# Flamingo-style gated cross-attention and local-attention layers on one core: four pairs ahead of the repeating step, and q's squares folded once on GpSimd

## Chip, cores and metric

One NeuronCore of one Trainium2 chip. The metric is the device time of one execution in microseconds, as the median of several runs. The fast TensorE level is 2.4 GHz, the other 1.2 GHz; the profile gives the granted clock as a share of full speed.

## What is computed

Sixteen sequences `x[b]` of 128 tokens by 128 values go through a gated cross-attention and then, regrouped, through a two-layer block of local attention and feed-forward; the block's change is scaled by a second gate. Cut to what matters:

```python
# cross-attention, one head, per sequence, over 120 context rows of 96 values
a = layernorm(x); c = layernorm(ctx)
p = softmax((a@Wq+bq) @ (c@Wk+bk).T * 128**-0.5)
x = x + tanh(g_xattn) * ((p @ (c@Wv+bv)) @ Wo + bo)
# block: the sequence is normalised and transposed, then two layers of
h = shift_token(x);  q, k, v = split(h @ wqkv)            # 8 heads of 64
q, k = l2norm(q)*qs, l2norm(k)*ks;  q, k = rotary_xpos(q, k)
x = x + local_attention(q, k, v) @ wo                      # window 64
h = layernorm(shift_token(x));  a, g = split(h @ w1 + b1)
x = x + (a * gelu(g)) @ w2 + b2
```

`l2norm` divides each head's 64 values by the root of the sum of their squares: 16 sums (8 heads of q, 8 of k) per token.

## The kernel before

Everything lies in SBUF. The work is in units of one sequence in one layer, called a batch here: `m.i` from 0 to 31, the layer is `m.i // 16`. Buffers of a batch come in twos, by `m.i % 2`. The feed-forward works on groups of four batches (the last four in two groups of two), the cross-attention on pairs of sequences, eight in all.

Five engine programs (SP only loads and stores) run each in its own queue and in its own order, and meet by semaphores. Each has a function `step(s)`, called for `n` from -168 to 58, and in it a list of conditions, the order of which is the order of the queue. `s.on(d)` means that batch `n + d` exists; `s.pair(d)` gives a pair every other step, but only from pair `XP` on; `s.group(d)` a group every fourth step. What belongs to the pairs below `XP`, and to the last two groups, stands in lines of its own with a number (`if s.n == -25`). The number serves only to place the call in the queue: a call of step -25 runs as soon as its engine and its semaphores allow.

A batch goes through these functions (engine, line of the work):

- TensorE `project_k`, `project_q`, `project_v` (L505 to L507): h times the weights as a high and a low part, three matmuls of 512 columns each, into PSUM. `wqkv_hi` is made by ScalarE (`weights_high`, L1006), `wqkv_lo` by GpSimd (`weights_low`, L355). `h_hi` is a cast on VectorE (`token_high`, L1322; `group_high`, L1328), `h_lo` a subtraction on GpSimd (`token_low`, L392).
- ScalarE `squares(m, s)` (L1059) squares q (s=0) or k (s=1) into `sqr`. VectorE `turns(m, s)` (L1355, L1358) makes the two rotary products from PSUM, GpSimd `rotate(m, s)` (L410) adds them.
- VectorE `squared(m, s)` (L1365) sums the squares per head: 128x512 to 128x8. GpSimd `clamped(m)` (L423) limits the 16 sums from below, ScalarE `lengths(m)` (L1063, L1065) makes `rr`, their inverse roots. GpSimd `unit_k(m)` (L417) scales k by them; q's go in with the mask.
- TensorE `rows_q` (L634), `rows_k` (L644) transpose; ScalarE `q_rows` and VectorE `k_rows` (L1387) copy out; TensorE `scores_` (L661); VectorE `maxima_(m, a)` (L295 as its first mark, then L1376) scales, masks and takes row maxima; ScalarE `weights(m, a)` (L1071) the exponentials; VectorE `inverse`, GpSimd `normalise(m, a)` (L403), TensorE `weights_T` (L677), ScalarE `weights_out` (L1076), TensorE `attend` (L689) and `out_proj` (L698), VectorE `attn_residual`.
- Per group: `deviation`, `variance`, six `hidden` matmuls (L730), ScalarE `gelu` (L1102), VectorE `gate` (L1410), TensorE `back` (L780), VectorE `update`.

In step n VectorE sums q's squares of batch n+3 (`squared(s.at(3), 0)`) and k's of batch n+4; GpSimd does `unit_k(n+2)`, `rotate(n+2, 0)`, `rotate(n+3, 1)`, `clamped(n+3)`, `normalise(n+1, 0)` and `normalise(n+1, 1)`, with the cross-attention's parts between.

A pair of the cross-attention goes through: VectorE `stats(p)` (L1252), ScalarE `norms(p)` (L1011 to L1014), `tokens_normed` and `context_normed` (VectorE for pairs 0 and 1: L1277, L1284; GpSimd for the others: L375, L365), TensorE `tokens_T`, `context_T`, ScalarE `tokens_affine` (L1018), `context_affine`, then `query_in`/`query_out`, `context_scores`, VectorE `maxima(p)` (L1296), ScalarE `context_exps` (L1032), `values_in`/`values_out`, `probs_T`/`probs_out`, `mix`, VectorE `context_sums`, `residual`, ScalarE `norm_out`, `stack_in` (VectorE or GpSimd, L385), TensorE `out_T`, ScalarE `results`, then `token_high` and `token_low`, after which the pair's two batches can be projected. `weights_folded` (L486 to L489) and VectorE's `folded` (L1263) join the cross-attention's weights once; four `bias_fold` calls (L497, six matmuls of one column each) put the layernorm's bias through w1.

PSUM's eight banks are shared by all. Ahead of a matmul that writes a bank, `passed(semaphore, value)` waits for its last reader.

The parts of `XP` = 2 pairs stand in numbered lines; pairs 2 to 7 run in the repeating lines from step -19 (`stats`) to step 8. ScalarE needs two function tables; before, `gelu_and_others` is loaded ahead of a group's three gelus (L1199) and `natural_log_exp_and_others` right behind them (L1212).

Of the kernel before, what the change touches and what calls it, by code (L numbers as in the profile page):

```python
# [27 lines left out]
ALU = mybir.AluOpType  # L28
# [6 lines left out]
INNER = HEADS * DH  # L35
# [7 lines left out]
XP = 2  # L43
# [53 lines left out]
def build(nc, x, ctx_768, bo, wqkv, q_scale, k_scale, w1, wo, w2, packed, rot, mask, ident, out):  # L97
    ctx = ExitStack()
    with ctx:
# [87 lines left out]
        TT_B, CT_B, QI_B, VI_B, SC_B, PX_B, MI_B, OX_B = (TQ, TQ, SB), (OB, VB, VB), (SB, KB, KB), (SB, QB, VB), (TK, TQ, TQ), (OB, TQ, SB), (OB, KB, TK), (SB, TK, TQ)  # L187
# [6 lines left out]
        ld_x = [sem(f"ld_x{k}") for k in range(3)]  # L194
        ld_c = [sem(f"ld_c{k}") for k in range(3)]
# [19 lines left out]
        q_ps, k_ps, v_ps = (sem(n) for n in ("q_ps", "k_ps", "v_ps"))  # L215
        sqq_done, sqk_done, redq_done, redk_done, ss_ready, ln_done, r_ready = (
# [57 lines left out]
        FIRST, LAST = -168, 58  # L274
# [32 lines left out]
        XCH = CCH = ((0, 2), (2, 8), (8, 16))  # L307
# [3 lines left out]
        def _(sp):  # L311
# [24 lines left out]
        def _(pool):  # L336
            pool.dma_start(bo_s[:], bo.rearrange("(o d) -> o d", o=1)).then_inc(ld_b, 16)
            pool.dma_start(rott[:], rot).then_inc(ld_small, 16)
# [19 lines left out]
            def context_normed(p):  # L358

                pool.wait_ge(x_rs, 3 * p + 3)  # L360
                if p == XP:
                    pool.wait_ge(x_zc, XB * XP)
# [5 lines left out]
            def tokens_normed(p):  # L368

                pool.wait_ge(x_rs, 3 * p + 3)  # L370
                if p == XP:
                    pool.wait_ge(x_z, XB * XP)
# [5 lines left out]
            def stack_in(p):  # L378

                pool.wait_ge(x_rs2, 2 * p + 2)  # L380
                if p == XP:
                    pool.wait_ge(x_z2, XB * XP)
# [28 lines left out]

            def unit_k(m):
# [12 lines left out]
            def step(s):  # L425
                if s.n == -1:
                    weights_low(0, 2)
                if s.on(2):
                    unit_k(s.at(2))
                if s.pair(7) is not None:  # L430
                    stack_in(s.pair(7))
                if s.on(2):
                    rotate(s.at(2), 0)
                if s.pair(14) is not None:
                    tokens_normed(s.pair(14))
                if s.n == 8:
# [3 lines left out]
                if s.pair(13) is not None:  # L440
                    context_normed(s.pair(13))
                if s.n == -8:
                    token_low(0)
                if s.pair(6) is not None:
                    token_low(s.pair(6))
                if s.n == -63:
                    tables_(0)
                if s.on(3):
                    rotate(s.at(3), 1)
# [1122 lines left out]
```

## Time and profile before

| what | value |
|---|---|
| median of 3 runs | 400.29 us |
| lowest and highest run | 395.24, 403.95 us |
| the profiled execution | 399.71 us |
| its span in the profile | 397.9 us |
| TensorE, VectorE, ScalarE, GpSimd busy | 90%, 84%, 78%, 59% |

The span goes from the first to the last instruction that the profile shows; the profiled execution took 1.8 us more. PE is TensorE, PEld its weight loads, DVE VectorE, ACT ScalarE, POOL GpSimd. A line such as `26.26 0.26 DVE L1322 CAST h_hi<-xs ...` gives start, duration, engine, line of the kernel, operation, output and input; in brackets stands the idle time of the engine ahead of it and what ended it.

### The profile page before, as it was taken

To read this page: it belongs to the slowest core of one execution; us is meant where nothing else is said; L and a number is where in the kernel's file an instruction comes from. 1 tells how busy PE (TensorE), PEld (TensorE's weight loads), DVE (VectorE), ACT (ScalarE), POOL (GpSimd) and SP (SyncE) were. 2 spreads that over 40 slices of the span, in tenths; PEclk is the share of its full clock that TensorE was granted. 3 is DMA by queue.
4 is the path that set the end of the run, shared out by engine and by line. 5 is a ranking of instruction groups with operands and counts; after the bars stand their busy time and mean duration, and the time that the engine had idled before them with its cause. 6 is when DMAs were issued, how large, how long until landed. Compare 5 with 4: busy or idle time off the path is not lost.

```text
span 397.9 us, 8200 instructions
## 1 busy us (share of the span) xinstructions
PE 359.7 (90%) x2502; PEld 263.1 (66%) x2502; DVE 336.0 (84%) x1286; ACT 308.4 (78%) x976; POOL 235.3 (59%) x260
## 2 busy tenths in 40 slices
PE   2888669899999999999999999999999999999895
PEld 1676548677776767667666677667666766666663
DVE  3697797999986999998899889998999889975535
ACT  3575658898989879986897689868986898678852
POOL 2197777797756659757564755575557554662200
PEclk9966888999999999999999999999999999999999
DMA  8900000000000000000000000000000000000001
GB/s 227 331 4 0 2 1 2 2 2 2 2 1 2 0 2 0 2 2 1 2 0 2 2 2 2 1 2 1 2 2 0 2 1 2 29 0 2 27 2 53
DMA packets 3472, 7.14 MB, mean 18 GB/s; under 512 B 403, under 2 KB 1973, under 8 KB 3429
## 3 DMA queue, kind: packets, MB, share of 16 engines
q1 hardware_dynamic: 3005, 6.13, 4.6%
q0 software_dynamic: 144, 0.26, 0.4%
q8 instruction: 21, 0.34, 0.4%
q10 hardware_dynamic: 279, 0.22, 0.2%
q14 instruction: 23, 0.18, 0.1%
HBM read 5.57 MB, written 1.05 MB: 17 GB/s over the span
## 4 chain that ended last, share of the span: by engine, by line
PE 64%; DVE 19%; ACT 7%; issue 6%; DMA 2%; POOL 1%; SPq 0%; DVEq 0%; POOLq 0%
PE ps L730 8%; PE ps L689 7%; PE ps L698 6%; PE ps L661 5%; PE ps L780 5%; PE ps L677 4%; PE ps L505 4%; PE ps L507 4%; PE ps L506 4%; DVE pp L1376 3%; PE ps L644 3%; DVE sn L1358 3%; PE ps L634 3%; DVE cs L1355 3%; ACT pT L1076 2%
## 5 line engine op out<-in xcount | busy, mean ns | idle before, releaser
L1071 ACT ACTIVATE pp<-pp,nm 128x128 f32<-128x128 f32 x256 | 99.1, 392 | 3.0 <-DVE nm L1376 2.8
L410 POOL TENSOR_TENSOR cs<-cs,sn 128x512 f32<-128x512 f32 x64 | 82.2, 1299 | 0.0
L403 POOL TENSOR_TENSOR pp<-pp,pri 128x512 f32<-128x512 f32 x64 | 66.7, 1042 | 16.5 <-DVE pri L1383 14.3
L1376 DVE CUSTOM_DVE_ANT_0 pp<-ps,msk,rr 128x128 f32<-128x128 f32 x256 | 74.3, 346 | 0.4
L423 POOL TENSOR_SCALAR ssc<-ss 128x16 f32<-128x16 f32 x32 | 7.9, 248 | 99.9 <-DVE ss L1365 99.9
L1076 ACT ACTIVATE pT<-ps 128x512 f32<-128x512 f32 x64 | 34.8, 596 | 36.2 <-PE ps L677 36.1
L1071 ACT ACTIVATION_READ_ACCUMULATOR pp<-pp,nm 128x1 f32 x256 | 49.0, 191 | 0.0
L730 PE MATMUL ps<-hn,w1g 128*128 128x512 f32 (+3 forms) x108 | 47.8, 555 | 1.2 <-DVE sn L1358 0.9
L505 PE MATMUL ps<-wqkv_hi,h_hi 128*128 128x512 f32 x96 | 45.9, 478 | 2.7 <-DVE sn L1358 2.4
L1358 DVE TENSOR_TENSOR sn<-ps,stab 128x256 f32<-128x256 f32 x128 | 47.6, 413 | 0.0
L661 PEld LDWEIGHTS ps<-kT,qT 64*128 64x128 f32 x512 | 31.9, 191 | 21.9 <-issue 15.8
L1355 DVE TENSOR_TENSOR cs<-ps,ctab 128x512 f32<-128x512 f32 x64 | 43.9, 686 | 2.9 <-ACT sqr L1059 1.4
L689 PE MATMUL ps<-pT,vv 128*64 128x128 f32 x512 | 35.0, 277 | 8.9 <-ACT pT L1076 8.6
L1365 DVE TENSOR_REDUCE ss<-sqr 128x8 f32<-128x512 f32 x64 | 42.5, 665 | 0.0
L689 PEld LDWEIGHTS ps<-pT,vv 128*64 128x64 f32 x512 | 28.2, 136 | 21.2 <-issue 21.2
L1059 ACT ACTIVATE sqr<-ps 128x512 f32<-128x512 f32 x64 | 37.6, 588 | 3.6 <-PE ps L507 2.7
L661 PE MATMUL ps<-kT,qT 64*128 64x128 f32 x512 | 38.1, 289 | 1.5 <-DVE kT L1387 1.4
L507 PE MATMUL ps<-wqkv_hi,h_lo 128*128 128x512 f32 x96 | 38.9, 405 | 0.0
L506 PE MATMUL ps<-wqkv_lo,h_hi 128*128 128x512 f32 x96 | 38.8, 405 | 0.0
L698 PEld LDWEIGHTS ps<-oT,wo_raw 128*128 128x128 f32 x256 | 32.5, 192 | 7.0 <-issue 6.2
L417 POOL TENSOR_TENSOR cs<-cs,rr 128x512 f32<-128x512 f32 x32 | 33.5, 1048 | 2.9 <-ACT rr L1065 2.7
L677 PE MATMUL ps<-idn,pp 128*128 128x128 f32 x256 | 35.0, 279 | 0.2 <-ACT gl L1102 0.2
(132 smaller groups left out, 750.5 us busy)
## 6 DMA issues: line engine op xcount, KB each, us to landing
wqkv_raw<-in_L_ffn_wqkv_dram SPq DMA_DIRECT2D x2, 768.0 KB, 12.8
out_dram<-xt SPq DMA_DIRECT2D x3, 256.0 KB, 2.4
w_raw<-in_w_dram SPq DMA_DIRECT2D x1, 682.0 KB, 13.0
xt<-in_x_dram SPq DMA_DIRECT2D x1, 512.0 KB, 9.2
wo_raw<-in_wo_dram SPq DMA_DIRECT2D x1, 512.0 KB
xt<-in_x_dram SPq DMA_DIRECT2D x1, 384.0 KB, 6.4
ct<-in_ctx_dram SPq DMA_DIRECT2D x1, 360.0 KB, 10.0
ct<-in_ctx_dram SPq DMA_DIRECT2D x1, 270.0 KB, 6.8
```

The lines of the kernel that those rows point to most:

```text
L403: T(pp[m.j][:, a, :, :], pp[m.j][:, a, :, :], pri[m.j][:, a * 4:a * 4 + 4].unsqueeze(2).to_broadcast([128, PAIRS, 128]), ALU.mult).then_in ...
L410: T(cs[m.j][:, part], cs[m.j][:, part], sn[m.j][:, part], ALU.add).then_inc((aq_done, ak_done)[s], 1)
L505: mm(ps[:, part, :], hi, whi, start=True, stop=False)
L507: mm(ps[:, part, :], lo, whi, start=False, stop=True).then_inc((q_ps, k_ps, v_ps)[part], 1)
L661: last = mm(ps[:, SA + a, c * 128:(c + 1) * 128], qT[m.j][r, c, :], kT[m.j][r, c, :], start=True, stop=True)
L689: last = mm(ps[a * 64:a * 64 + 64, OB, c * 128:(c + 1) * 128], vv[m.j][:, h * DH:(h + 1) * DH], pT[m.j][:, a, c, :], start=True, stop=True)
L698: last = mm(ps[:, OB, Y], wo_raw[:, m.layer, c, :], oT[m.j][:, c, :], start=(c == 0), stop=(c == PAIRS - 1))
L730: mm(ps[0:m, bank, t.w], w1g[:, layer, s * HID + o:s * HID + o + m], hg, start=True, stop=True).then_inc((ha_ps, hg_ps)[s][c], 1)
L1071: A(pp[m.j][:, a, c, :], pp[m.j][:, a, c, :], ACT.Exp, bias=nm[m.j][:, a * 4 + c:a * 4 + c + 1], scale=-1.0, accum_out=psum_[m.j][:, a * 4 ...
L1355: V.tensor_tensor(heads(cs[m.j], s), x_, ctab[:, m.layer, s, :].unsqueeze(1).to_broadcast([128, HEADS, DH]), ALU.mult)
L1358: last = V.tensor_tensor(heads(sn[m.j], s)[:, :, o_], x_[:, :, i_], stab[:, m.layer, s, o_].unsqueeze(1).to_broadcast([128, HEADS, 32]), A ...
L1376: last = V.tensor_tensor_reduce(out=pp[m.j][:, a, c, :], in0=ps[:, SA + a, c * 128:(c + 1) * 128], in1=msk[:], scale=rr[m.j][:, h:h + 1], ...
```

## The change

It has five parts.

1. `XP` goes from 2 to 4, so that pairs 2 and 3 too stand in numbered lines. The order of the numbered lines is new on all engines, the PSUM banks of the pairs are new (a fifth set of banks for the repeating lines), and with them the `passed` waits: eight go, one comes ahead of `rows_q`, and the numbered lines have others. `VP = 2` keeps the split between VectorE and GpSimd at pair 2.

```diff
-XP = 2
+XP = 4
-        FIRST, LAST = -168, 58
+        FIRST, LAST = -155, 58
...
             def rows_q(m):
                 pe.wait_ge(aq_done, m.i + 1)
                 passed(pt_ready[0], min(m.i - 1, ALL))
+                passed(qT_ready, min(m.i, ALL))
                 passed(x_out, 2 * pairs_by(m.i + 5))
                 passed(x_p, XB * pairs_by(m.i + 6))
```

2. The loads: chunks of 1, 1, 2 and 4 pairs instead of 1, 3 and 4; SP and GpSimd wait for the first pair before they issue the rest; wqkv of layer 0 goes ahead of the last chunk.

```diff
+        VP = 2
-        XCH = CCH = ((0, 2), (2, 8), (8, 16))
+        XCH = CCH = ((0, 2), (2, 4), (4, 8), (8, 16))
...
-            for k in range(1, 3):
+            sp.wait_ge(ld_x[0], 16)
+            sp.wait_ge(ld_c[0], 16)
+            for k in range(1, 4):
+                if k == 3:
+                    sp.dma_start(wqkv_raw[:, 0, :], wqkv[0]).then_inc(ld_w[0], 16)
                 sp.dma_start(*rows(xt, x, XCH[k])).then_inc(ld_x[k], 16)
                 sp.dma_start(*rows(ct, ctx_768, CCH[k])).then_inc(ld_c[k], 16)
-            sp.dma_start(wqkv_raw[:, 0, :], wqkv[0]).then_inc(ld_w[0], 16)
...
             pool.dma_start(bo_s[:], bo.rearrange("(o d) -> o d", o=1)).then_inc(ld_b, 16)
+            pool.wait_ge(ld_c[0], 16)
             pool.dma_start(rott[:], rot).then_inc(ld_small, 16)
```

3. The fold. GpSimd adds the upper 32 squares of each head of q to the lower 32, in place, and VectorE sums 32 values per head: 128x256 to 128x8. k's sums stay as they are.

```diff
+            def squares_folded(m):
+                pool.wait_ge(sqq_done, m.i + 1)
+                q = sqr[m.j][:, 0:INNER].rearrange("p (h d) -> p h d", d=DH)
+                T(q[:, :, 0:DH // 2], q[:, :, 0:DH // 2], q[:, :, DH // 2:DH], ALU.add).then_inc(fold_q, 1)
...
             def squared(m, s):
-                dve.wait_ge((sqq_done, sqk_done)[s], m.i + 1)
-                V.tensor_reduce(ss[m.j][:, s * HEADS:(s + 1) * HEADS], heads(sqr[m.j], s), AX.X, ALU.add).then_inc(
+                dve.wait_ge((fold_q, sqk_done)[s], m.i + 1)
+                sq = heads(sqr[m.j], s)
+                V.tensor_reduce(ss[m.j][:, s * HEADS:(s + 1) * HEADS], sq if s else sq[:, :, 0:DH // 2], AX.X, ALU.add).then_inc(
                     (redq_done, redk_done)[s], 1)
```

4. GpSimd's step has the fold of batch n+3 behind `rotate(n+2, 0)`; the three `weights_low` of layer 1 go from step 8, ahead of `rotate(n+3, 1)`, to step 11, behind it. `context_normed` of pairs 4 to 7 is two steps later than before (`pair(13)` to `pair(11)`), `stats` one (`pair(24)` to `pair(23)`), VectorE's `w1_in(1)` goes from step 13 to 9. The orders near the loop's start, after the change (a few of the calls, with their step):

```
GpSimd   -155 tables_(0)  -25 tokens_normed(2)  -18 context_normed(2)  -12 weights_low(0,1)
         -10 weights_low(0,0) token_low(0) weights_low(0,2)  -9 context_normed(3)  -8 tables_(1)
         -6 tokens_normed(3)  -5 tokens_normed(4) token_low(1)  -3 squares_folded(0) tokens_normed(5) rotate(0,1) clamped(0)
         -2 unit_k(0) stack_in(2) rotate(0,0) squares_folded(1) context_normed(4) rotate(1,1) clamped(1)
VectorE  -50 stats(0)  -45 centring() folded()  -44 tokens_normed(0)  -35 context_normed(0)  -29 stats(1)
         -2 turns(1,0) bias_sum turns(2,1) squared(1,0) k_rows(0) token_high(2) squared(2,1)
         -1 maxima(3) maxima_(0,0) turns(2,0) maxima_(0,1) ... 
ScalarE  -77 norms(0)  -68 norms(1)  -51 tokens_affine(0)  -50 context_affine(0)  -46 query_out(0)
TensorE  -6 bias_fold(0,0) bias_fold(0,1) out_T(1)  -5 project_k(0)
```

Before, VectorE has `stats(0)`, `stats(1)`, `tokens_normed(0)` in step -43, and in step -2 `k_rows(0) squared(2,1) token_high(2)`; GpSimd has `weights_low(0,2)` first in step -1.

5. ScalarE's table loads come from a helper: `table(name)` loads only when the other table is in, ahead of the next function that needs it. Behind a group's gelus the load of the logarithm's table now stands behind `squares(n+4, 1)` and ahead of `weights`.

## Rows read from the trace of the kernel before

**Rows 1.** The page, part 1: busy time of each engine, share, instructions.

```profile
PE 359.7 (90%) x2502; PEld 263.1 (66%) x2502; DVE 336.0 (84%) x1286; ACT 308.4 (78%) x976; POOL 235.3 (59%) x260
```

**Rows 2.** Stages: stretch, length, busy PE, PEld, DVE, ACT, POOL; PE clock, DMA share, GB/s.

```profile
20.00:40.00 20.00, 16.77 (x70) 14.21 (x71) 16.70 (x76) 12.62 (x44) 16.38 (x26) 0.64 0.01 2
40.00:60.00 20.00, 12.94 (x73) 10.02 (x72) 17.68 (x56) 12.42 (x44) 15.52 (x18) 0.84 0.00 1
65.00:105.00 40.00, 37.02 (x326) 30.67 (x327) 38.85 (x161) 35.95 (x130) 32.53 (x38) 1.00 0.01 2
...
246.74:286.90 40.16, 39.24 (x283) 27.73 (x283) 36.83 (x136) 32.77 (x105) 24.30 (x26) 1.00 0.00 1
```

**Rows 3.** Groups by line; count, busy us, mean ns, idle us before, releaser.

```profile
L1365 DVE TENSOR_REDUCE ss<-sqr 128x8 f32<-128x512 f32 x64 | 42.5, 665 | 0.0
...
L417 POOL TENSOR_TENSOR cs<-cs,rr 128x512 f32<-128x512 f32 x32 | 33.5, 1048 | 2.9 <-ACT rr L1065 2.7 <-issue 0.2
...
L1199 ACT ACT_TABLE_LOAD x7 | 9.0, 1283 | 0.1
...
L423 POOL TENSOR_SCALAR ssc<-ss 128x16 f32<-128x16 f32 x32 | 7.9, 248 | 99.9 <-DVE ss L1365 99.9
...
L392 POOL TENSOR_TENSOR h_lo<-xs,h_hi 128x256 fp32r<-128x256 f32 x8 | 5.4, 681 | 1.4 <-DVE h_hi L1322 1.4
...
L1296 DVE TENSOR_REDUCE nmx<-ps 128x2 f32<-128x240 f32 x8 | 3.2, 403 | 3.4 <-PE ps L581 3.4
```

**Rows 4.** DMA issues: count, KB each, median us from issue to landing.

```profile
wqkv_raw<-in_L_ffn_wqkv_dram SPq DMA_DIRECT2D x2, 768.0 KB, 12.8
...
idn<-in_identity_dram SPq DMA_DIRECT2D x1, 64.0 KB, 3.3
```

**Rows 5.** Timeline from 6 to 30 us: start, duration, instruction, idle before.

```profile
6.50 0.74 PE L489 MATMUL ps<-bo_s,hot 1*97 1x128 f32 x2
...
9.03 0.29 DVE L1252 BATCH_NORM_STATS2 bst<-xt 128x6 f32<-128x128 f32 x1 [2.87 <-DMA ct<-in_ctx_dram]
...
10.17 0.57 DVE L1277 TENSOR_SCALAR hn<-xt,mv,r 128x128 f32<-128x128 f32 x2
...
10.80 0.20 ACT L1014 ACTIVATE r<-lnv 128x4 f32<-128x4 f32 x1
...
11.58 0.56 ACT L1018 ACTIVATE x1T<-ps,first 128x256 f32<-128x256 f32 x1 [0.58 <-PE ps L551]
...
18.06 1.14 ACT L1006 ACTIVATE wqkv_hi<-wqkv_raw 128x512 fp32r<-128x512 f32 x2
...
29.31 0.78 PE L505 MATMUL ps<-wqkv_hi,h_hi 128*128 128x512 f32 x1
```

**Rows 6.** Timeline, VectorE's two casts and what follows the second.

```profile
26.26 0.26 DVE L1322 CAST h_hi<-xs 128x256 fp32r<-128x256 f32 x1
...
48.52 3.60 DVE L1322 CAST h_hi<-xs 128x256 fp32r<-128x256 f32 x1
...
50.67 1.29 POOL L410 TENSOR_TENSOR cs<-cs,sn 128x512 f32<-128x512 f32 x1
...
51.93 1.64 POOL L375 TENSOR_SCALAR hn<-xt,mv,r 128x128 f32<-128x128 f32 x2
...
57.06 1.09 PE L634 MATMUL ps<-idn,cs 128*128 128x128 f32 x4 [1.57 <-ACT xp L1032]
...
63.30 0.06 DVE L295 MEMSET mark_v<- 128x1 f32 x1 [1.49 <-PE ps L661]
```

**Rows 7.** Timeline of GpSimd: clamped in two early steps, and a middle step.

```profile
88.68 0.25 POOL L423 TENSOR_SCALAR ssc<-ss 128x16 f32<-128x16 f32 x1
...
97.91 0.25 POOL L423 TENSOR_SCALAR ssc<-ss 128x16 f32<-128x16 f32 x1 [2.64 <-DVE ss L1365]
...
259.29 2.51 POOL L410 TENSOR_TENSOR cs<-cs,sn 128x512 f32<-128x512 f32 x2
...
264.14 0.24 POOL L423 TENSOR_SCALAR ssc<-ss 128x16 f32<-128x16 f32 x1 [2.34 <-DVE ss L1365]
```

More of the change, by code:

```diff
@@ L431, in step @@
                     stack_in(s.pair(7))
+                if s.n == 0:
+                    stack_in(3)
+                if s.n == -10:
+                    weights_low(0, 0)
+                if s.n == -2:
+                    stack_in(2)
+                if s.n == -8:
+                    tables_(1)
+                if s.n == -1:
+                    token_low(2)
                 if s.on(2):
                     rotate(s.at(2), 0)
+                if s.on(3):
+                    squares_folded(s.at(3))
+                if s.pair(6) is not None:
+                    token_low(s.pair(6))
+                if s.n == -10:
+                    token_low(0)
+                if s.pair(11) is not None:
+                    context_normed(s.pair(11))
+                if s.n == -6:
+                    tokens_normed(3)
+                if s.n == -25:
+                    tokens_normed(2)
+                if s.n == -9:
+                    context_normed(3)
                 if s.pair(14) is not None:
                     tokens_normed(s.pair(14))
-                if s.n == 8:
+                if s.n == -12:
+                    weights_low(0, 1)
+                if s.on(3):
+                    rotate(s.at(3), 1)
+                if s.n == -18:
+                    context_normed(2)
+                if s.n == -155:
+                    tables_(0)
+                if s.n == 11:
                     weights_low(1, 0)
@@ L1109, in step @@
                 if s.n == 51:
-                    nc.scalar.preload_act_table_set("gelu_and_others")
                     gelu(8, 0)
+                if s.n == -10:
+                    weights_high(0, 2)
                 if s.n == -8:
-                    results(0)
+                    norms(3)
+                if s.n == -7:
+                    norm_out(1)
                 if s.on(4):
@@ L1174, in step @@
                     gelu(7, 0)
+                if s.n == -46:
+                    query_out(0)
+                if s.n == -1:
+                    norm_out(3)
                 if s.n == 58:
                     gelu(8, 2)
+                if s.n == -27:
+                    context_affine(1)
+                if s.n == -8:
+                    results(0)
+                if s.n == -51:
+                    tokens_affine(0)
                 if s.pair(10) is not None:
@@ L1488, in step @@
                     context_sums(s.pair(8))
+                if s.n == 0:
+                    token_high(3)
                 if s.on(1):
                     inverse(s.at(1), 1)
+                if s.n == -1:
+                    context_sums(3)
+                if s.n == -11:
+                    stack_in(1)
+                if s.n == -3:
+                    context_sums(2)
+                if s.n == -44:
+                    tokens_normed(0)
+                if s.n == -8:
+                    token_high(1)
+                if s.n == -3:
+                    residual(2)
+                if s.n == -2:
+                    token_high(2)
+                if s.n == -1:
+                    residual(3)
                 if s.on(4):
@@ L1494, in step @@
                     normed_h(7)
+                if s.n == -19:
+                    maxima(1)
                 if s.n == 45:
                     result(7)
[L1497 to L1498 removed]
                 if s.pair(7) is not None:
                     token_high(s.pair(7))
[L1501 to L1505 removed]
+                if s.n == 9:
+                    w1_in(1)
+                if s.n == -50:
+                    stats(0)
                 if s.pair(8) is not None:
```

440 lines of the change are left out of this document (248 added, 192 removed).

## The prediction

> **What bounds the kernel now.** I read the page first: TensorE is busy 90% of the span, VectorE 84%, ScalarE 78%, GpSimd 59% [rows 1]. An average over the span says little here, so I cut the span into stages [rows 2]. In the repeating step far from both ends (246.74 to 286.90 us, four steps in 40.16 us) TensorE is busy 39.24 us: only 0.92 us of four steps is not matmul, while VectorE has 3.3 us and GpSimd nearly 16 us free; the granted clock is 1.00. That stage, some twenty steps, is bound by TensorE. From 65 to 105 us it is the other way round: VectorE 38.85 of 40 us, TensorE 37.02. There the cross-attention pairs lie on top of the step and VectorE is the bound. From 20 to 60 us nobody is full: TensorE 29.7 of 40 us at a granted clock of 0.64 and 0.84, VectorE 34.4, and part of VectorE's time is not work, as shown below. So the change can earn in three places, in this order: the crossing into the loop (20 to 65 us), the VectorE-bound steps, and least in the long middle.
>
> **The fold, per step.** VectorE's sum over 512 values takes 665 ns; the nearest smaller sum is over 240 values, 403 ns [rows 3]. That is (665-403)/272 = 0.96 ns per value, so 256 values are 0.42 us and one sum saves 0.25 us, 32 times: 7.9 us of VectorE's busy time. GpSimd gets 32 new additions of 128x256. The nearest row is the other two-input operation of that size, L392, 681 ns; half of L417 (1048 ns) gives 0.52, and a strided access could make it as dear as a 128x512 addition, 1.26 us (2.51 for two [rows 7]). I take 0.66 us: 21 us more for GpSimd, from 235 to 256 us.
>
> Is the fold hidden? It stands behind unit_k and rotate(q), ahead of rotate(k). In a middle step GpSimd ends both rotates at 259.29+2.51 = 261.80 and then sits until 264.14, 2.34 us, for VectorE's sum [rows 7]; over the run that wait is 99.9 us in 29 of 32 steps, 3.4 us each [rows 3]. The squares are ready a step earlier, so the fold would end at about 261.2 and VectorE's sum, now at about 263.4, does not wait for it. Its cover is that idle time; without it 0.66 us would stand ahead of VectorE's sum, and behind that on VectorE the inverses and copies for which TensorE waits. In steps where GpSimd also has stack_in and context_normed the cover is gone: at 88.68 clamped starts with no wait, as GpSimd has only just ended its rotate [rows 7], so there it comes up to 0.7 us later.
>
> What does 0.25 us give? In the VectorE-bound stage, 65 to 105 us, up to its full size: four steps, 1.0 us (bounds 0 and 2.0, if all eight steps with pairs give it). In the middle only what TensorE's idle time allows: 0.92 us per four steps is an upper end of 5.5 us over 24 steps, but VectorE is not what the matmuls mostly wait for there; I take 0.1 us per four steps, 0.6 us (bounds 0 and 5.5).
>
> **The start of the loads.** SP now waits for the first pair's two loads. Behind that wait stand all other x and ctx chunks, the weights, the mask and later the stores; behind GpSimd's new wait stand the three small loads for the tables. The first pair's data are there at about 4.5 to 4.9 us, so pairs 1 to 3 and wqkv are asked for then and not at 1.6 to 3.5 us. The landing of a small load was 3.3 us after its issue [rows 4], so pair 1 is there at about 8.2 us; now its statistics start at 9.03 after 2.87 us of waiting for ctx [rows 5]. No loss. The first wqkv took 12.8 us to land; issued at 6.3 us instead of 3.5 and still taking that long, it would land at 19.1, and ScalarE reads it at 18.06 [rows 4, 5]: at worst 1.0 us late. But 874 KB of x and ctx now come behind it, so I take 0. The x and ctx of pairs 4 to 7 and w1, behind it, are first used after 20 us, mask and wo after 50.
>
> VectorE's order gains more on paper: tokens_normed(0) no longer stands behind stats(1) and can follow folded, whose matmuls end at 6.50+0.74 = 7.24 us. With 0.85 us for folded it starts at 8.1 instead of 10.17: 2.1 us [rows 5]. But ScalarE's queue takes it back. norms(1) stands ahead of tokens_affine(0) there, before and after the change, and it needs stats(1), which VectorE now does after context_normed(0), from 9.3 us. From stats(1) to the last of norms(1) it is 9.03 to 11.00 now, 1.97 us, so tokens_affine(0) starts at about 11.3 instead of 11.58. I take 0.3 us (bounds -1.0 and 3.1, the wait of 2.87 and a little earlier landing).
>
> From there to the first project_k (29.31) I find nothing that adds up. out_T(0) comes about 1 us earlier, since norm_out(0) is no longer behind norms(2) and probs_out(1). But results(0) now has weights_high(0,2), norms(3) and both affines of pair 2 ahead of it on ScalarE, and two bias folds stand directly ahead of project_k(0).
>
> **The crossing into the loop.** Two things stand out. First, VectorE's cast token_high(2) at 48.52 took 3.60 us; the same cast at 26.26 took 0.26 [rows 6]. During the 3.34 us between, VectorE does nothing and GpSimd runs without a gap (weights_low(0,2), unit_k, rotate), until tokens_normed at 51.93. VectorE's next work, the first masked maxima, starts when the cast ends, and TensorE stands behind that. In the new order weights_low(0,2) is done long before, and the cast comes before squared(2,1) while GpSimd is about to wait for the lengths. I expect a stall of about 1.1 us there, the rest of context_normed and rotate: gain 2.2 us (bounds 0 and 3.3).
>
> The Trainium skill, SBUF — State Buffer, in Who interferes with whom, says that a cast in a two-port mode and a GpSimd instruction exclude each other for one whole instruction, whoever came first, and that tensor_reduce never contends. By it the cast would wait for one GpSimd instruction, at most 1.3 us, and the gain of this term would be 2.0 us or more; the row, in which three GpSimd instructions went by, gives the lower end 0. The page speaks against the change as a whole, since every fold is one more holder of the pair.
>
> Second, rows_q(1) waited at 57.06 for the exponentials of pair 3 (the 1.6 us idle before it), and TensorE then ran at the lower of its two levels: its four transposes took 1.09 us and VectorE waited 1.49 us at 63.30 for the scores [rows 6]. With four pairs ahead this wait does not exist for pair 3, and maxima(3) goes before maxima_(0). I take 1.2 us (bounds 0 and 1.5). The bank changes and the added wait on qT_ready ahead of rows_q hit buffers long free: 0. results(3), ahead of rows_q(2), I put at 0 too (at most the 1.6 us that such a wait cost at 57.06).
>
> **Small moves.** The three weights_low of layer 1 (1.26 us each, 3.8 in all) go from step 8 to step 11, between rotate(k) and clamped, where GpSimd has 2.34 us less 0.66 free: clamped, and with it lengths and both normalise, come up to 2.1 us late once. I take a loss of 0.4 us (bounds 0 and 2.1). w1_in(1) and the pairs' stats move on engines with room: 0. ScalarE's table loads stay as many, each at its first user, where squares now precede the load: 0, with a rival below.
>
> **The sum.** 0.3 + 2.2 + 1.2 + 1.0 + 0.6 - 0.4 = 4.9 us. The profiled execution took 399.71 us (span 397.9 and 1.8 around it), which gives 394.8; from the median of the runs, 400.29, it would be 395.4. I forecast **395.0 us**. The runs themselves lie from 395.24 to 403.95, so about 2% (8 us) is what a measurement can tell from no change.
>
> **The rivals.**
> A, the forecast: 395.0, its own range 391.5 to 398.5. Chance 0.50.
> B, the loop begins earlier by the whole of what the front has: the 3.1 us of the front, 3.3 of the cast, 1.5 of the wait at 63.30, 2.0 of the folds, less 0.4: 9.5 us, 390.2. For it: TensorE's slow clock in 20 to 40 us stretches each delay, and a fuller front could lift it [rows 2]. Against it: norms(1) on ScalarE, and GpSimd, 16.38 of 20 us busy from 20 to 40 us, with weights_low(0,2), a second table and a fold more ahead of the first rotate. Chance 0.22.
> C, given back: the loop starts some microseconds earlier, and GpSimd, with 32.53 + 4 x 0.66 = 35.2 of 40 us, becomes late in the steps with pairs: clamped comes late, lengths behind it on ScalarE holds the squares, and the steps lose what the front won. About 399.7. For it: 88.68. Against it: in the step after, at 97.91, it waits 2.64 us again, and a pair spans two steps. Chance 0.17.
> D, slower: VectorE waits in its queue for the fold. In the twelve steps -3 to 8 the fold is not hidden: 12 x 0.66 = 7.9 us plus the 0.4, against 0.3 + 3.4 + 0.6 from the front and middle: +4.0, 403.7. It decides where GpSimd has less than 0.66 us idle before clamped in these steps. With a fold of 1.26 us it would be 15.1 in place of 7.9, 410.9. Chance 0.08.
> E, the change does not do what it says on ScalarE: squares now run with the gelu table loaded, which no row of before shows, so a load may be put ahead of them and another for the exponentials. Seven places at 1.28 us [rows 3] are 9.0 us; on the path they give 399.7 - 4.9 + 9.0 = 403.8. Chance 0.03.
> The Trainium skill, ScalarE: Activation LUTs, in What ACT_TABLE_LOAD costs, puts a switch at 2.66 us with its drain, which would make E's seven places 18.6 us (an estimate), and in Table sets names relu, copy, identity and abs as part of every set, not square.
>
> **Range and chances.** B's centre must be inside and D's too: 389.0 to 402.5 leaves about 2 in 10 out. Faster by over 2% means under 392.3: most of B and a little of A, 0.25. Slower by over 2% means over 408.3: D with the dear fold and mishaps not listed, 0.05. Within 2%: 0.70.
>
> **What would show it.** Right: sums of q at about 0.42 us and folds at about 0.66; four middle steps still in about 40 us with TensorE busy 39.2; token_high(2) under 1.5 us; no wait ahead of rows_q(1); the first maxima_ of batch 1 near 59.5 instead of 63.34. x1T of pair 0 near 11.3 tells A from B. Wrong: sums of q that wait for fold_q (D), ScalarE holding more than seven loads of each kind at the gelus (E), clamped without any wait in most early steps and 65 to 105 us holding no more work than now (C), or a middle cycle far from 40 us, since then TensorE was not the bound that I take it for.

## The result and the profile after

The changed kernel takes 394.72 us in the median of 20 runs (393.16 to 398.06), against 399.25 us for the kernel before in 20 runs on the same chip (394.67 to 405.3). The ratio is 0.994, with a 95% interval from 0.991 to 0.997: a small gain, inside the 2% that counts as no change. (The ratio leaves out runs over 1.5% above the fastest of their kernel, seven of the 20 before and none after, so it speaks of 2.4 us where the medians speak of 4.5.) The profiled executions are 393.99 us (span 392.2) after and 399.71 us (span 397.9) before.

Part 1 of the page after, busy time by engine, answers to [rows 1]:

```profile
PE 354.7 (90%) x2502; PEld 259.2 (66%) x2502; DVE 330.2 (84%) x1286; ACT 307.1 (78%) x976; POOL 257.2 (66%) x292
```

The groups by line (count, busy us, mean ns, idle before and its releaser), beside [rows 3]:

```profile
L1487 DVE TENSOR_REDUCE ss<-sqr 128x8 f32<-128x512 f32 x64 | 34.0, 531 | 0.0
...
L422 POOL TENSOR_TENSOR sqr<-sqr 128x256 f32<-128x256 f32 x32 | 23.5, 735 | 0.0
...
L1443 DVE CAST h_hi<-xs 128x256 fp32r<-128x256 f32 x8 | 12.5, 1568 | 0.2 <-ACT xs L1138 0.2
...
L435 POOL TENSOR_SCALAR ssc<-ss 128x16 f32<-128x16 f32 x32 | 8.2, 255 | 74.5 <-DVE ss L1487 74.4
```

VectorE's sums fell from 42.5 to 34.0 us: the 32 sums of k still take about 0.66, those of q 0.40 to 0.41. GpSimd has 32 additions of 0.735 us more and its idle time ahead of clamped went from 99.9 to 74.5 us, that is by about the folds. But VectorE's busy time fell by 5.8 us only and not by 8.5. The third line has the reason: the eight casts take 12.5 us together, where they took 8.1 before. Their mean of 1.57 us hides that two take nearly 4.5 us and the other six 0.26 to 0.91. (Some smaller VectorE work became about 2 us shorter.)

The stages after (columns as in [rows 2]):

```profile
20.00:40.00 20.00, 15.85 (x71) 13.10 (x72) 16.16 (x74) 12.94 (x42) 18.26 (x25) 0.67 0.13 47
40.00:60.00 20.00, 15.81 (x126) 12.43 (x125) 18.22 (x76) 15.55 (x56) 18.80 (x23) 0.99 0.01 2
...
65.00:105.00 40.00, 36.57 (x288) 29.69 (x286) 38.72 (x149) 33.79 (x121) 33.70 (x40) 0.96 0.00 1
246.74:286.56 39.82, 38.99 (x284) 27.69 (x282) 35.78 (x134) 32.69 (x105) 27.15 (x29) 1.00 0.01 1
```

From 40 to 60 us TensorE does 2.9 us more than before, at a clock of 0.99 in place of 0.84. From 65 to 105 us it does 0.5 us less, at 0.96 in place of 1.00. Four middle steps are 39.82 us, 0.34 less than the four of [rows 2], which contained a slow one; other groups of four differ by 0.2.

The best ruler for the rest is the start of the scores matmuls of each step (L661 before, L685 after). The span falls into five stretches:

| from the traces, us | before | after | difference |
|---|---|---|---|
| start to scores(3) | 81.41 | 73.11 | -8.30 |
| scores(3) to (8) | 52.40 | 57.99 | +5.59 |
| scores(8) to (16) | 83.21 | 81.79 | -1.42 |
| scores(16) to (31) | 148.94 | 148.13 | -0.81 |
| scores(31) to the end | 31.92 | 31.18 | -0.74 |
| span | 397.9 | 392.2 | -5.7 |

A step is named here by the scores at its end: step 5 runs from scores(4) to (5). The code's own numbers, which some of the expectations use, are three lower. Most of what the start wins is lost again in steps 5 (9.90 us before, 13.30 after) and 7 (12.77 and 15.15). The timeline of the first of these, after (start, duration, instruction, idle before and its releaser; here and below, lines of other work that stand between are left out):

```profile
81.22 2.05 POOL L409 TENSOR_TENSOR pp<-pp,pri 128x512 f32<-128x512 f32 x2
...
81.86 4.47 DVE L1443 CAST h_hi<-xs 128x256 fp32r<-128x256 f32 x1
83.22 1.06 POOL L429 TENSOR_TENSOR cs<-cs,rr 128x512 f32<-128x512 f32 x1
84.22 1.29 POOL L416 TENSOR_TENSOR cs<-cs,sn 128x512 f32<-128x512 f32 x1
85.45 0.73 POOL L422 TENSOR_TENSOR sqr<-sqr 128x256 f32<-128x256 f32 x1
86.26 0.60 DVE L1520 TENSOR_TENSOR xs<-ps,xs 64x128 f32<-64x128 f32 x2
86.41 0.72 POOL L398 TENSOR_TENSOR h_lo<-xs,h_hi 128x256 fp32r<-128x256 f32 x1 [0.23 <-DVE h_hi L1443]
...
87.00 1.09 PE L713 MATMUL ps<-pT,vv 128*64 128x128 f32 x16 [2.13 <-DVE xs L1520]
...
88.20 0.40 ACT L1158 ACTIVATE pp<-pp,nm 128x128 f32<-128x128 f32 x1 [2.69 <-DVE nm L1498]
```

Read it from the cast. It is issued inside GpSimd's first normalise, and stays until GpSimd comes to rest: both normalise, unit_k, rotate and the new fold go by. GpSimd rests only because token_low needs the result of this very cast. TensorE then waits 2.13 us for VectorE's residual and ScalarE 2.69 us for the next maxima. The same happens at 104.05, 4.49 us. In the kernel before the casts of those pairs took 0.79 and 0.78 us, and the long one was that of [rows 6].

### The profile page after: what moved, and what is told of

The parts are those of the page before. It is cut to its first block, busy times and chain, and to the rows that moved or that the text cites. A ratio compares the mean times of both kernels' runs of the same rounds, so it can differ in the third digit from the quotient of the medians.

```text
span 392.2 us, 8237 instructions
## 1 busy us (share of the span) xinstructions
PE 354.7 (90%) x2502; PEld 259.2 (66%) x2502; DVE 330.2 (84%) x1286; ACT 307.1 (78%) x976; POOL 257.2 (66%) x292
## 4 chain that ended last, share of the span: by engine, by line
PE 64%; DVE 17%; issue 8%; ACT 8%; POOL 1%; DMA 1%; ACTq 0%; DVEq 0%; POOLq 0%
PE ps L754 10%; PE ps L713 7%; PE ps L722 6%; PE ps L685 5%; PE ps L804 5%; PE ps L536 4%; PE ps L701 4%; PE ps L537 4%; PE ps L538 4%; PE ps L668 3%; PE ps L659 3%; DVE sn L1479 2%; DVE pp L1498 2%; ACT pT L1163 2%; DVE cs L1476 2%
## 5 line engine op out<-in xcount | busy, mean ns | idle before, releaser
L435 POOL TENSOR_SCALAR ssc<-ss 128x16 f32<-128x16 f32 x32 | 8.2, 255 | 74.5 <-DVE ss L1487 74.4
L685 PEld LDWEIGHTS ps<-kT,qT 64*128 64x128 f32 x512 | 31.1, 187 | 21.1 <-issue 11.3
L685 PE MATMUL ps<-kT,qT 64*128 64x128 f32 x512 | 37.2, 285 | 0.7 <-ACT qT L1171 0.5
L1487 DVE TENSOR_REDUCE ss<-sqr 128x8 f32<-128x512 f32 x64 | 34.0, 531 | 0.0
```

Of the source, the lines that this page charges most:

```text
L685: last = mm(ps[:, SA + a, c * 128:(c + 1) * 128], qT[m.j][r, c, :], kT[m.j][r, c, :], start=True, stop=True)
```

## The experiments

The runs came in three batches and one single run, each on a chip of its own. The kernel before ran in each, at 399.47, 400.0, 400.12 and 397.58 us. Medians of different batches can differ by that much without a cause in the kernel; the stretches between scores are the finer measure. Each ratio is to the kernel before of the same batch.

**The changed kernel again.**

> The changed kernel itself, as the yardstick of this batch. Its profile is expected at 392 to 394 us of span, ahead of the kernel before by about 8 us at the scores of batches 3 and 4, and with the casts token_high(4) and token_high(5) at about 4.5 us each instead of 0.8. If these two long casts were an accident of one execution, one or both are 0.8 us here and the span is 3 us shorter for each.

395.23 us in 10 runs, ratio 0.994 (0.990 to 0.998). The long casts come again, 4.45 us at 83.76 and 4.47 at 105.92. They are no accident of one execution.

**The fold alone.** The kernel before, with the fold behind rotate of q and nothing else of the change:

```diff
             def squared(m, s):
-                dve.wait_ge((sqq_done, sqk_done)[s], m.i + 1)
+                dve.wait_ge((fold_q, sqk_done)[s], m.i + 1)
...
                 if s.on(2):
                     rotate(s.at(2), 0)
+                if s.on(3):
+                    squares_folded(s.at(3))
```

> The kernel before with the fold alone. If the fold is worth what VectorE gains in the VectorE-bound steps and 0.2 to 0.3 us per four middle steps, it gains 1 to 3 us against before. Rival 1: in the early steps the fold makes GpSimd's queue gapless and VectorE's casts starve more often; then one or more token_high casts are over 3 us long and the gain is lost, 0 to +6 us. Rival 2: the fold does nothing to the time, within 0.5 us.

399.02 us in 10 runs, ratio 1.0036 (1.0001 to 1.0071): the fold alone gains nothing and rather costs a little. Its timeline has two long casts where the kernel before has one:

```profile
67.03 4.12 DVE L1331 CAST h_hi<-xs 128x256 fp32r<-128x256 f32 x1
...
88.86 4.46 DVE L1331 CAST h_hi<-xs 128x256 fp32r<-128x256 f32 x1
```

The long cast of [rows 6] is gone: that cast takes 0.32 us here, the small scaling after it 0.56 us, and the step from scores(0) to (1) 10.96 us in place of 12.80. The cast at 67.03 lengthens step 3 from 10.54 to 12.79 us instead. From scores(3) to (8) it needs 55.58 us, 3.18 more than before; from (8) to (31) 1.15 less. So the fold does gain 0.2 to 0.3 us in one step of four, and pays for it with each cast that it sets back.

**The change without the fold.** VectorE sums 64 values of q again, the rest of the change stays:

```diff
-                if s.on(3):
-                    squares_folded(s.at(3))
...
-                dve.wait_ge((fold_q, sqk_done)[s], m.i + 1)
+                dve.wait_ge((sqq_done, sqk_done)[s], m.i + 1)
```

> The changed kernel without the fold: sums over 64 values again. If the whole gain is the new order and the w1_in move, it stays at the changed kernel's time plus 1 to 3 us. If the fold is what starves the casts of pairs 4 and 5, those two casts fall to 0.8 us and it is 1 to 4 us faster than the changed kernel. If the starving comes from the order of the other GpSimd work, the casts stay at 3.5 us or more, shorter than 4.5 only by the fold's 0.7.

390.05 us (389.48 to 390.21, 4 runs), ratio 0.982 (0.977 to 0.987). No cast is longer than 0.79 us, and scores(3) to (8) takes 52.47 us, as before. With the result above it says that the order, the loads, w1_in(1) and the table loads together are worth about 9 us by the medians (7 by the ratio), and that the fold takes about 5 of them back: from scores(3) to (8) it is 5.5 us.

**The casts on ScalarE.** The changed kernel with its fold; ScalarE does the casts of pairs 4 to 7 behind heads_out:

```diff
+            def token_high(p):
+                act.wait_ge(x_out, 2 * p + 2)
+                at = slice(p * XB, p * XB + XB)
+                A(h_hi[:, at, :], xs[:, at, 0:N], ACT.Copy).then_inc(xh_hi, 1)
```

> The changed kernel with the casts of pairs 4 to 7 on ScalarE. If the long casts cost what the trace suggests (3.4 us in step 3's matmuls and 2.4 in step 5's), it is 4 to 6 us faster than the changed kernel, 389 to 391 us, and stays 8 us ahead of before until the scores of batch 7. Rival: VectorE's lost time is caught up later because TensorE is the bound from step 4 on; then it gains under 1 us.

389.79 us (388.53 to 390.39, 4 runs), ratio 0.981 (0.976 to 0.987). On ScalarE a cast takes 0.41 us, with GpSimd at work beside it, and steps 5 and 7 are 10.11 and 12.77 us. So it is VectorE's casts and not GpSimd's extra work as such: GpSimd does the same 32 folds here.

**GpSimd's order alone.** Nothing is added or taken away; token_low, which waits for the cast, goes from behind the fold to the head of GpSimd's step:

```diff
             def step(s):
+                if s.pair(6) is not None:
+                    token_low(s.pair(6))
                 if s.on(2):
                     unit_k(s.at(2))
...
-                if s.pair(6) is not None:
-                    token_low(s.pair(6))
```

> The kernel after, with one change: in GpSimd's step token_low(pair) stands first, ahead of unit_k, rotate of q and the fold, so that GpSimd comes to wait for VectorE's cast four instructions earlier. Nothing is added or removed. If a cast gets through only when GpSimd's queue comes to rest, the two casts of 4.5 us (pairs 4 and 5) end right behind the two normalise instructions, at 1.5 to 2.5 us each, and the kernel gains 3 to 5 us: 390 to 392 us. If a cast needs a fixed time or a given number of GpSimd instructions whatever the order, they stay at 4.4 us or more and the time stays at 394 to 396. If GpSimd becomes late by the wait, its sums of halves and clamps come later and steps 2 and 4 stay long with short casts: also 394 or more, but VectorE then waits at the sums of q.

389.01 us (388.61 to 390.08, 4 runs), ratio 0.975 (0.966 to 0.983). The cast arrives at the same place as after (81.87, in the first normalise) and ends with the second, as the first theory said:

```profile
81.23 2.03 POOL L409 TENSOR_TENSOR pp<-pp,pri 128x512 f32<-128x512 f32 x2
...
81.87 1.54 DVE L1443 CAST h_hi<-xs 128x256 fp32r<-128x256 f32 x1
...
83.49 0.73 POOL L398 TENSOR_TENSOR h_lo<-xs,h_hi 128x256 fp32r<-128x256 f32 x1 [0.23 <-DVE h_hi L1443]
84.18 1.04 POOL L429 TENSOR_TENSOR cs<-cs,rr 128x512 f32<-128x512 f32 x1
```

This is the clearest of the runs: same work, same arrival, and three instructions of GpSimd fewer in the run behind it make the cast 2.9 us shorter. From scores(3) to (8) it takes 52.96 us in place of 57.99, so the one moved call gains 5 us in this stretch. By the medians it is 6 us, somewhat more than expected, but these come from two batches.

**The same with five rounds, and its twin without the fold.** Both were run to price the fold where no cast is held for long.

> The version with token_low first on GpSimd once more, unchanged (389.01 us there), beside the one without the fold below. It should stand at 388.5 to 389.8, both casts at 1.5 to 1.6 us again. If the cast's length depends on where in GpSimd's run it happens to arrive and not on the order, one of the two can be back at over 3 us.

389.2 us (388.54 to 389.96, 6 runs), ratio 0.976 (0.973 to 0.979); the casts 1.53 and 1.57 us.

> token_low first on GpSimd, and no fold (VectorE sums 64 values of q again): the fold's own worth where the casts do not starve. The fold shortens one step in four of the middle by 0.18 to 0.2 us and steps 20, 24, 29 and a few of the early ones likewise, some 1.5 us of the span in all; so without it 390.0 to 391.0 us, 1 to 2 above the version with the fold. If GpSimd's extra 23.5 us of work cost as much as they save, both are within 0.5 us of each other.

390.94 us (389.65 to 391.98, 6 runs), ratio 0.980 (0.976 to 0.984). The medians say that the fold is worth 1.7 us. The stretches say 0.68: 0.48 lost from scores(3) to (8), 0.47 and 0.69 won in the two after that. The rest lies ahead of scores(3), where executions differ among themselves. So the sign is the expected one and the size is between 0.6 and 1.7 us.

**No fold, casts on ScalarE.** The version with the ScalarE casts, less the fold:

> The kernel after without the fold (VectorE sums 64 values of q again) and with the casts of pairs 4 to 7 on ScalarE behind heads_out. The fold is priced where nothing starves. If a hidden fold is worth the 0.12 us that each sum loses in the steps that VectorE bounds, this stands 0.5 to 2 us above the version with the ScalarE casts and the fold (389.8 us), at 390.3 to 391.8, with steps 20, 24 and 29 at 10.32 to 10.46 in place of 10.1 to 10.3. If the fold costs even there, through GpSimd's chain or the port, it stands under 389.5. Moving the casts alone, without the fold, should do nothing against the version without the fold (390.05): they took 0.4 to 0.8 us there.

391.75 us (389.37 to 392.65, 4 runs), ratio 0.980 (0.972 to 0.988). From scores(3) to (31) it is 283.42 us, against 282.82 with the fold: 0.6 us for the fold again. Its median is 1.7 us above the version without the fold whose casts stayed on VectorE, which the stretches do not show (283.42 against 283.60); four runs with a spread of 3.3 us can't tell.

**Less the waits at the loads.** From that version, the waits on the first pair's loads ahead of the later ones go:

```diff
-            sp.wait_ge(ld_x[0], 16)
-            sp.wait_ge(ld_c[0], 16)
...
-            pool.wait_ge(ld_c[0], 16)
             pool.dma_start(rott[:], rot).then_inc(ld_small, 16)
```

> The version of this call without the fold and with the ScalarE casts, less the three waits ahead of the later loads (SyncE no longer waits for the first pair of x and of the context before it issues the next pieces, GpSimd no longer waits before it issues the tables). If the early start comes from the first pieces having the DMA queues to themselves, stats(1), the first tokens_affine and x1T come 0.8 to 1.5 us later (x1T near 11.5 in place of 10.5) and the whole becomes 0.5 to 1.5 us longer. If it comes from the order of VectorE's and ScalarE's instructions alone, x1T stays within 0.3 us of 10.5 and the time within 0.3 us.

390.02 us (389.1 to 391.85, 4 runs), ratio 0.977 (0.970 to 0.984). x1T of pair 0 starts at 10.70 instead of 10.48, within the 0.3 us of the second theory, so its early start comes from the order. On the whole time these runs say little: the median fell by 1.7 us, in a spread of 3 us, while in the profiled execution scores(3) came 2.6 us later, with the clock lower from 40 to 60 us (0.83 against 1.00). From scores(3) to (31) the two agree within 0.13 us. No gain from the waits is shown. The new chunks of the loads, and wqkv ahead of the last one, were not undone in any run.

**w1_in(1) back in the code's step 13.** The base is again the version with neither the fold nor VectorE's casts:

```diff
-                if s.n == 9:
-                    w1_in(1)
...
+                if s.n == 13:
+                    w1_in(1)
```

> The version of this call without the fold and with the ScalarE casts, with w1_in(1) back in VectorE's step 13 as in the kernel before. If the w1_in of step 13 is what makes step 16 long (11.26 us before against 10.12 after), step 16 grows by 0.9 to 1.3 us here, step 9 or its neighbours shrink by at most 0.3, and the time grows by 0.7 to 1.2 us. If w1_in is covered wherever it stands (that is how it was predicted, at nothing), step 16 grows by under 0.3 and the time does not move.

Step 16 grows from 10.32 to 11.25 us, the size of the first theory, and its row says how:

```profile
198.41 1.58 DVE L1467 TENSOR_SCALAR w1g<-w_raw,first 128x682 f32<-128x682 f32 x1
...
202.51 0.30 PEld L752 LDWEIGHTS ps<-hn,w1g 128*128 128x128 f32 x2 [1.10 <-DVE sn L1485]
```

The median, 390.48 us (390.11 to 390.91, 4 runs), is not above that of its base (391.75), so 0.93 us is shown by the steps alone, and the expected growth of the whole time is not. From scores(8) to (16) it is 82.62 against 81.67, and every kernel of this study with w1_in(1) in the code's step 13 has the long step 16 (11.25 or 11.26 us, 10.91 with the fold alone; 10.12 to 10.33 in the others).

**The one cast of the kernel before.** The kernel before, with the cast of pair 2 on ScalarE behind heads_out:

```diff
                 if s.on(0):
                     heads_out(s.at(0))
+                if s.pair(7) == 2:
+                    token_high(2)
```

> The kernel before, with one instruction moved: the cast of pair 2, which took 3.60 us on VectorE at 48.52, is done by ScalarE behind heads_out of that step. If that cast is the greater part of what the crossing into the repeating steps gained (6.6 us from scores(0) to scores(1), by the traces before and after), the step from scores(0) to scores(1) falls from 12.80 us to 9.3 to 10.5 and the whole gains 2.2 to 3.3 us: 396 to 397 where before is at 399.5. If the gain came from the order of pairs 2 and 3 and of the last exps, whose waits stand right behind the cast, the step loses under 1 us and the time stays within 1 us of before.

399.26 us (395.99 to 403.21, 12 runs), ratio 0.9975 (0.993 to 1.002). The first theory fails, and what the second one said came: the step loses 0.94 us, and the time stays within 1 us of the kernel before in its batch (400.12). The cast takes 0.42 us on ScalarE and maxima_(0) goes ahead at 48.21, but the next VectorE instruction of this kind takes over the stall. It is the scaling of two columns for the pair's softmax, 0.17 us by itself:

```profile
52.04 0.72 POOL L392 TENSOR_TENSOR h_lo<-xs,h_hi 128x256 fp32r<-128x256 f32 x1
52.10 1.91 DVE L1306 TENSOR_SCALAR nmb<-nmx 128x2 f32<-128x2 f32 x1
52.72 1.26 POOL L410 TENSOR_TENSOR cs<-cs,sn 128x512 f32<-128x512 f32 x1
...
54.04 0.36 ACT L1032 ACTIVATE xp<-ps,nmb 128x120 f32<-128x120 f32 x1 [2.86 <-DVE nmb L1306]
...
54.98 0.30 PE L634 MATMUL ps<-idn,cs 128*128 128x128 f32 x1 [3.31 <-ACT xp L1032]
```

rows_q(1) now waits 3.31 us for the exponentials of pair 3, where it waited 1.57 in [rows 6]. The step from scores(0) to (1) falls from 12.80 to 11.86 us only. Two stalls lay one behind the other. In the changed kernel both are small: 0.91 us for the cast, and no wait ahead of rows_q(1). No run takes both away in the old order by themselves. The nearest is the fold alone, where both were short by the time at which they came, and this step took 10.96 us.

**Both remedies at once.** token_low first and the casts on ScalarE:

> Both remedies at once: the casts of pairs 4 to 7 on ScalarE and token_low first in GpSimd's step. If what was left of the casts (1.5 us twice) is still on the path, step 5 falls from 10.66 to about 9.9 to 10.1 us and the time to 388.2 to 388.8, 0.5 to 1 below token_low first alone (389.1). If TensorE or ScalarE sets the end of those steps, the two remedies do not add and it stands at 388.8 to 389.8.

389.18 us (388.53 to 392.28, 7 runs), ratio 0.980 (0.977 to 0.984). Step 5 falls from 10.66 to 10.07 us and step 9 from 11.85 to 11.35, but steps 4, 6 and 8 grow by 0.3 each: scores(3) to (8) is 53.24 against 52.96. The remedies do not add. From scores(3) to (31) the three versions with the fold and a remedy stand within 0.13 us: 282.89 with token_low first, 282.82 with the casts on ScalarE, 282.77 with both. token_low first is the smallest edit, at 389.0 and 389.2 us, ahead of both kernels.

## Why the prediction was right, and where its steps were not

The time came out at 394.72 for a forecast of 395.0. The nearness is luck, since two errors cancel: the start won more than the sum said, and a loss of 5.5 us was not in it. The gain itself, forecast at 4.9 us, is 4.5 by the medians, 2.4 by the ratio and 5.7 in the profiled pair.

**The front, 0.3 us.** Too low. x1T of pair 0 started at 10.52 and not at 11.3:

```profile
8.65 0.28 DVE L1373 BATCH_NORM_STATS2 bst<-xt 128x6 f32<-128x128 f32 x1
...
10.52 0.55 ACT L1101 ACTIVATE x1T<-ps,first 128x256 f32<-128x256 f32 x1
...
27.18 0.78 PE L536 MATMUL ps<-wqkv_hi,h_hi 128*128 128x512 f32 x1
...
44.38 0.91 DVE L1443 CAST h_hi<-xs 128x256 fp32r<-128x256 f32 x1
```

The mechanism (ScalarE's norms(1) holds x1T back until stats(1)) was right: from stats(1) to x1T it is 1.87 us. The term was mis-sized because stats(1) started at 8.65 and not from 9.3, with no wait for ctx; folded took 0.50 us where the working had 0.85. "Nothing that adds up" between there and project_k(0) was wrong too: that came at 27.18 instead of 29.31, 1.1 us more than x1T explains. By scores(0) the profiled pair is 3.6 us apart (44.72 against 48.27). The worst-sized term of the sum is this one. (The working's 874 KB behind wqkv are 512 and 360, so 872; nothing hangs on it.) The sentence that x1T near 11.3 tells A from B spoke for B, rightly: this part went as in B.

**The crossing, 2.2 + 1.2 us.** The cast took 0.91 us, under the 1.5 of the prediction, rows_q(1) has no wait, and maxima_ of batch 1 came at 56.15 where I had said 59.5 and the kernel before has 63.34. In the profiled pair the start to scores(3) is 8.3 us shorter against the 3.7 of the three terms. Of the 8.3, 3.6 lie ahead of scores(0) and 4.7 behind it, where the two crossing terms had 3.4. Part of this is the two executions: TensorE's granted clock was 0.50 from 56.5 to 63 us before and 1.00 after. The other kernels tell more: scores(3) came between 72.74 and 76.54 us in the eleven profiled executions with the new order (mean 74.0), and at 81.41, 80.11 and 78.25 in the three with the old one (mean 79.9). So the new order with its loads is worth about 6 us, some 2.8 ahead of scores(0) and 3.1 from there to scores(3). That is an estimate from few executions, and two of the three old ones hold a change of their own: the fold's held cast costs the second 2.2 us in step 3, and the moved cast helps the third. By it the two crossing terms together were right in size, and the front term was 2.5 us too small. The split into 2.2 for the cast and 1.2 for the wait behind it did not hold. The cast alone gives 0.9 us in its step, since the next stall takes over; that both together give the rest is argued from the traces, not shown by a run.

**The fold in the steps that VectorE bounds, 1.0 us.** This step failed. The fold costs 5.5 us there in the changed kernel (57.99 us from scores(3) to (8), 52.48 without it), where even the lower bound was 0. It costs 3.2 us in the old order. I put the fold's cover at GpSimd's idle time, found that time gone in steps with pairs, and priced it as clamped coming up to 0.7 us later. The price was not there but at VectorE: GpSimd's run without rest became the time that the cast waits. [rows 6] had the mechanism in it, a cast of 3.60 us over three GpSimd instructions, and the text counted only its disappearance at the crossing, not that it could come back elsewhere. The prediction also remarked that every fold is "one more holder of the pair", and gave this neither a price nor a chance. TensorE's clock is not the cause of the loss: in the profiled execution it was 0.50 from 88.5 to 91.5 us, in the repeat 1.00 through the whole stretch, and the repeat takes 57.95 us there too. Even where no cast is held for long the fold does not gain in this stretch: it loses 0.3 to 0.5 us. Rival C named the stage and the size (what the front wins is given back), and its sign came true: clamped starts without a wait, or with one of 0.14 us, in seven of the first eight steps after, and in two before, and 65 to 105 us hold no more work. Yet its mechanism, clamped that comes late, is not the cause: with token_low first clamped stands in the same place (81.02 us against 81.00) with as little wait, and the loss is gone.

The Trainium skill, SBUF — State Buffer, in Who interferes with whom, has the kind of conflict: a cast or a tensor_scalar on VectorE and a GpSimd instruction exclude each other when the VectorE one runs in a two-port mode, for the whole instruction of whoever comes first. No trace shows the mode. The traces agree on which operations suffer (the cast here, the tensor_scalar of two columns in the run on the kernel before, never the sums, which took 0.64 to 0.68 us over 512 values in both kernels), and differ on the size: the cast waited over up to five GpSimd instructions, 4.2 us beyond its own 0.26, where one instruction would have been 1.0.

**The fold in the middle, 0.6 us.** Right in kind and low by half: 0.2 us in one step of four, 1.15 us from scores(8) to (31) by the fold alone, 1.16 by the pair with token_low first. It is near the lower end of 0 to 5.5, as TensorE was the bound. The fold took 0.735 us against 0.66, the sum 0.41 against 0.42.

**The small moves.** The three weights_low of layer 1, taken at -0.4, cost nothing visible. w1_in(1), taken at 0, gives 0.93 us: in the code's step 13 it takes 1.58 us and TensorE waits for VectorE behind it, in step 9 it takes 1.00. The table loads, taken at 0 with a rival below it, give 0.74 us at the end. Both kernels have 19, two at the start and 17 in the steps, so E did not come. Before and after, the load ahead of the last group's variance (start, duration):

```profile
384.34 1.28 ACT L1195 ACT_TABLE_LOAD   x1
...
385.64 0.38 ACT L1089 ACTIVATE dsq<-ps 128x256 f32<-128x256 f32 x1
```

```profile
379.50 0.38 ACT L1176 ACTIVATE dsq<-ps 128x256 f32<-128x256 f32 x1
379.91 1.28 ACT L1079 ACT_TABLE_LOAD   x1
```

Before, the load stands between the gelus and the squares; after, the squares go first, and the matmul over them starts 1.1 us earlier counted from scores(31). That is read from the traces and the code; no run undid this part alone. The stretch behind scores(31) is 31.89 to 31.92 us in all three kernels with the old loads and 31.16 to 31.18 in all with the new ones.

**The sum as it was:** about 6 us from the order at the start (8.3 in the profiled pair), -5.6 from the casts (the pair's difference), 1.1 from the fold from step 8 on, 0.9 from w1_in(1), 0.74 from the table load at the end. That gives 3.1 by the mean of the starts and 5.4 in the profiled pair, where the spans differ by 5.7. The 4.5 of the medians and the 2.4 of the ratio lie on both sides of the first.

## What to carry to other kernels

When work moves to GpSimd, look for VectorE casts and small SBUF-only operations that are issued while GpSimd runs its two-input operations back to back; the cost lands on VectorE, and only the duration column shows it (a cast of 4.47 us where others have 0.26). Look for such a cast in the kernel before, too: it shows that the mechanism is there. If the cast's own consumer on GpSimd can go ahead of the run, its wait gives GpSimd the pause that lets the cast in; here that one moved call was worth 5 to 6 us, and the fold itself at most 1.7.

## What the runs showed of the hardware

A VectorE cast from SBUF to SBUF beside GpSimd's two-input operations can be passed over, not for one instruction, but until GpSimd pauses or comes to an operation of another kind. With the fold alone, the cast at 67.03 ended at 71.15, behind the fold and as GpSimd's tokens_normed, a TENSOR_SCALAR, began at 70.97; so did the cast of [rows 6].

Whether it is passed over goes with the time at which it is issued. In the traces of this study, 14 casts of pairs were issued 0.63 to 0.68 us before the end of such a GpSimd instruction that had another directly behind it: all 14 got in at that end and took 0.78 to 0.83 us, and the GpSimd instruction behind took 1.07 to 1.10 us. Nine were issued 0.39 to 0.43 us before such an end, one 0.04 us before it and one 1.18 us before it: all eleven missed it. Seven of them missed the following ones too; the four of the version with token_low first found GpSimd waiting at the next. In the version without the fold, casts on VectorE, that of pair 4 is one of the 14:

```profile
81.01 2.16 POOL L409 TENSOR_TENSOR pp<-pp,pri 128x512 f32<-128x512 f32 x2
82.52 0.79 DVE L1441 CAST h_hi<-xs 128x256 fp32r<-128x256 f32 x1
83.12 1.09 POOL L429 TENSOR_TENSOR cs<-cs,rr 128x512 f32<-128x512 f32 x1
```

So the fold did harm in two ways that the runs don't part fully: it is one more instruction in the run, and it shifted the cast against GpSimd from the second normalise to the first. What decides at the boundary stays open; 0.4 and 0.63 us are what was seen, not a rule. The kind of the instruction behind could be a rival to the time: it was the second normalise in ten of the eleven long cases and unit_k in 12 of the 14 short ones. The exceptions, two short casts ahead of a second normalise and the long one of [rows 6] ahead of unit_k, speak against it.

The executions of one kernel differ in the start: the profiled ones had a clock of 0.64 to 1.00 from 20 to 40 us and 0.74 to 1.00 from 40 to 60 us, and from scores(3) on the stretches of kernels with the same steps agree within 0.15 us. In the kernel before the time goes with the clock: it had runs from 394.8 us at a mean clock of 0.98 to 403.3 us at 0.96. The 20 runs of the changed kernel lie closer, from 393.2 to 398.1, and show no such tie: the longest had 0.987 and the shortest 0.983. What makes those differ stays open.
